# GRU graph layers on one core: preparation of tiles 4 to 7 spaced evenly and split, the last tiles' results written as x + m z h - m (z - 1) n, the last chain in halves

## The chip, the core and the metric

The kernel runs on 1 core of one Trainium2 chip. The metric is the device time of one execution in microseconds. Engines are named as in the profile: PE (TensorE), DVE (VectorE), ACT (ScalarE), POOL (GpSimd), SP (SyncE, which here only issues DMAs).

## What is computed

64 graphs of 128 nodes with 128 channels. The state starts as relu of a layer norm, five layers of a gated graph network follow, and the result is added to the input:

```python
h = jnp.maximum(_layernorm(x), 0.0)
A = (adj != 0)
for l in range(5):
    m = jnp.einsum('bnd,de->bne', h, weight[l])
    agg = jnp.einsum('bij,bid->bjd', A, m)
    gi = agg @ w_ih.T + b_ih;  gh = h @ w_hh.T + b_hh      # each split into r, z, n
    r = sigmoid(i_r + h_r);  z = sigmoid(i_z + h_z)
    n = tanh(i_n + r * h_n)
    h = (1.0 - z) * n + z * h
out = x + h * mask
```

## The kernel before

**Tiles and units.** A tile is 4 graphs side by side: 128 partitions (channels, or nodes) by 512 columns; there are 16. One tile through one layer is a unit; there are 80, in the order of the list `units`: groups of 4 tiles, and within a group layer by layer, so the same tile comes again 4 units later. `K` is a unit's number (0 to 79), `l` its layer, `t` its tile, `LAST` the last layer (4). Units 16 to 19, 36 to 39, 56 to 59 and 76 to 79 are last layers.

**What a unit does.** PE: three products of the state with the hidden weights (`ps_r`, `ps_z`, `ps_hn`), three of the aggregated state `s` with the folded input weights (`ps_r`, `ps_z`, `ps_in`), each as three fp16 matmuls of high and low parts, and 8 small matmuls for the next unit's aggregation (`ps_s`). ACT: `r` (L478), `z` (L484), `s_hi` of the next unit (L472), the high part of the last unit's state (L494), `n` by tanh (L488). DVE: `rhn` (L624), the sum in `ps_in` (L630), `s_lo` of the next unit (L618), then the new state in two operations (L636, L641). POOL: `zh`, the product z h (L816), and `state_low`, the low part of the last unit's state (L821). SP: a transpose of the new state's two halves, `nat<-hp` (L242), which the aggregation of the same tile's next layer reads. Each engine runs its own list in order; semaphores tie them together.

**Preparation.** Tiles 4 to 15 are prepared while others are computed. Tile `t` begins at unit `prep[t]`, and stage `s` of it runs in unit `prep[t] + s`, behind that unit's own work on each engine: 0 moments (DVE) and loads, 1 `aggregate` (DVE) and statistics `inverse_std` (POOL, four small operations), 3 and 4 `layernorm` in two pieces (ACT), 5 `natural_high` (ACT) and `natural_low` (POOL), 6 `split` (ACT, the copy to `halves`), the compare of a tile 4 to 7 (POOL) and two transposes (SP), 7 the compare of the others (DVE, `adjacency`), 8 and 9 `join` in two pieces (DVE). Two neighbours stand `gap` units apart. `prep` is 4, 7, 10, 13 for tiles 4 to 7 and 18, 23, ... 53 for 8 to 15. `v_high` and `v_low` of layers 3 and 4 (ACT, DVE) fall into units 6 and 10, and PE folds layer 4's weights behind unit 10.

**Ends.** Finished tiles are masked and added to x on POOL (`masked_result`, `final`) and stored by SP. For the last group DVE does the mask product (`masked_state`, L648) for units 76 to 78. The very last unit takes its products in the order z, r, hn, in, and computes x + m z h on POOL (`masked_last_h`, `kept_result`), and DVE subtracts m (z - 1) n (`masked_open`, `last_result`); ACT copies the mask to PSUM (`move_mask`) and issues the last store.

Of the kernel before, what the change touches and what calls it, by code (L numbers as in the profile page):

```python
# [5 lines left out]
ALU = mybir.AluOpType  # L6
# [21 lines left out]
FINISH = 3  # L28
STAGES = 10
# [7 lines left out]
def gnn_kernel(nc, x, xT, adj, mask_row, fold_lhs, w_ihT, w_hhT, bias_ih, bias_hh, ident, out):  # L37
# [10 lines left out]
    END = at[starts[-1], LAST]  # L48
# [25 lines left out]
    storing = {adds[t] + 1: t for t in ends}  # L74
    fetching = {ends[t] - FETCH: [t] for t in ends}
    fetching.setdefault(N - FINISH - FETCH, []).append(TILES - 1)

# [4 lines left out]
    with ExitStack() as ctx:  # L82
# [66 lines left out]
        ps_s, ps_t, ps_f = bank("ps_s"), bank("ps_t"), bank("ps_f")  # L149

# [64 lines left out]
        def _(sp):  # L215
# [16 lines left out]
            def transpose_halves(t):  # L232
                sp.wait_ge(split_done, t - FIRST + 1)
# [39 lines left out]
            for K in range(1, N + 2):  # L273
# [6 lines left out]
                if K in tile_at_stage[6]:  # L280
                    transpose_first(tile_at_stage[6][K])
                    transpose_halves(tile_at_stage[6][K])
                if K in storing:
                    store(storing[K])
                for t in fetching.get(K, ()):
                    load_ends(t)
            for f in range(FRING):
                sp.wait_ge(stored[f], 16 * len(range(f, TILES, FRING)))

        @block.tensor  # L290
        def _(pe):
# [24 lines left out]
            def h_products(K):  # L316
# [29 lines left out]
            def last_products(K):  # L346
                pe.wait_ge(s_lo_done, K + 1)
                s_product(K, 1, ps_z).then_inc(z_mm, 1)
                s_product(K, 0, ps_r).then_inc(r_mm, 1)
# [85 lines left out]
        def _(act):  # L435
# [26 lines left out]
            def split(t):  # L462

                act.wait_ge(h0_done, 2 * t + 2)
                if t - FIRST >= 2:
                    act.wait_ge(halves_loaded[t % 2], 16 * ((t - FIRST) // 2))
                nc.scalar.copy(halves[:, t % 2], h0[:, t % LN].bitcast(U16).rearrange("p (c b) -> p b c", b=2)).then_inc(
                    split_done, 1)
# [16 lines left out]

            def gate_n(K):
# [13 lines left out]
            def move_mask():  # L500

                f = (TILES - 1) % FRING
                act.wait_ge(ends_loaded[f], 32 * ((TILES - 1) // FRING + 1))
                act.wait_ge(s_lo_done, N)
                nc.scalar.copy(ps_s[:], mask_in[:, f]).then_inc(mask_moved, 1)
# [35 lines left out]
            for K in range(N):  # L541
# [8 lines left out]
                else:  # L550
                    gate_z(K)
                    gate_r(K)
                    move_mask()
# [368 lines left out]
```

## Time and profile before

| | |
|---|---|
| median of 3 runs | 371.98 us (371.85 to 372.28) |
| the profiled execution, its own time | 371.11 us |
| its span, first to last instruction | 369.2 us |
| busy: PE, DVE, ACT, POOL | 98%, 87%, 81%, 71% of the span |
| mean granted TensorE clock | 0.997 |
| HBM read, written | 17.57 MB, 4.19 MB |

The span is what the rows below lie in; the execution's own time is 1.9 us longer. A matmul's row shows 0.38 us for 512 columns, longer than the distance to the next, because matmuls are pipelined. In the rows, a bracket at the end gives the engine's idle time ahead of the instruction and what ended it.

### The profile page before, as it was taken

The page shows a single profiled execution, that of the slowest core. Times are in us where ns is not written, and L with a number is a line of the kernel's source. Part 1 is how long each engine was busy: PE and PEld are TensorE (multiplying, and loading weights), DVE is VectorE, ACT ScalarE, POOL GpSimd, SP SyncE. Part 2 cuts the span into 40 slices and gives each one's busy share as a digit, 9 for nine tenths or more (in the row PEclk, how much of TensorE's full clock was granted, in tenths as well). Part 3 has the DMA queues.
Part 4 walks back from the last instruction along what each step waited for, and adds up shares of the span by engine and source line. Part 5 has one row for each costly group of instructions (what it writes and reads, how often), then busy time and mean ns, then how long its engine had stood idle before and what let it go on. Part 6 is the DMA issues. An engine that isn't in the chain of part 4 may idle for free.

```text
span 369.2 us, 6528 instructions
## 1 busy us (share of the span) xinstructions
PE 360.0 (98%) x2125; PEld 181.1 (49%) x2125; DVE 322.8 (87%) x588; ACT 299.8 (81%) x495; POOL 263.6 (71%) x261
## 2 busy tenths in 40 slices
PE   7999999999999999999999999999999999999992
PEld 3455555544454555555545455555545555555541
DVE  4977898899889999999999999999998988787886
ACT  5997788998879988888877889899877767777753
POOL 3765758889578878787656878888756777755574
PEclk9999999999999999999999999999999999999998
DMA  8634443857662693939624384756834543349522
GB/s 245 211 59 86 115 97 76 170 126 151 152 115 45 147 180 78 228 68 200 169 42 105 64 197 85 164 123 158 151 94 112 130 99 59 89 100 231 124 57 85
DMA packets 108512, 46.03 MB, mean 125 GB/s; under 512 B 97728, under 2 KB 98112, under 8 KB 108480
## 3 DMA queue, kind: packets, MB, share of 16 engines
q1 hardware_dynamic: 108336, 45.37, 55.3%
q8 instruction: 17, 0.28, 0.3%
q10 hardware_dynamic: 144, 0.26, 0.2%
q14 instruction: 15, 0.12, 0.1%
HBM read 17.57 MB, written 4.19 MB: 59 GB/s over the span
## 4 chain that ended last, share of the span: by engine, by line
PE 90%; DVE 4%; DMA 2%; POOL 2%; issue 1%; ACT 1%; DVEq 0%; POOLq 0%
PE ps_r L293 9%; PE ps_z L294 9%; PE ps_z L293 9%; PE ps_r L294 9%; PE ps_z L295 9%; PE ps_r L295 9%; PE ps_s L366 5%; PE ps_s L367 5%; PE ps_in L295 4%; PE ps_hn L294 4%; PE ps_in L293 4%; PE ps_in L294 4%; PE ps_hn L295 4%; PE ps_hn L293 4%; DMA hp<-nat 1%
## 5 line engine op out<-in xcount | busy, mean ns | idle before, releaser
L816 POOL TENSOR_TENSOR zh<-z,h 128x512 f32<-128x512 f32 x80 | 101.9, 1273 | 81.4 <-ACT z L484 81.3
L478 ACT ACTIVATE r<-ps_r,b_sum,unscale 128x512 f32<-128x512 f32 x80 | 62.2, 778 | 37.9 <-PE ps_r L295 37.5
L488 ACT ACTIVATE ps_in<-ps_in,b_ih,unscale 128x512 f32<-128x512 f32 x80 | 60.1, 751 | 22.3 <-DVE ps_in L630 21.3
L821 POOL TENSOR_TENSOR hp<-h,hp 128x512 f16<-128x512 f32 x64 | 74.1, 1157 | 0.0
L624 DVE SCALAR_TENSOR_TENSOR rhn<-ps_hn,b_hn,r 128x512 f32<-128x512 f32 x80 | 59.8, 748 | 10.3 <-ACT r L478 9.8
L630 DVE TENSOR_TENSOR ps_in<-ps_in,rhn 128x512 f32<-128x512 f32 x80 | 56.0, 700 | 11.5 <-PE ps_in L295 6.7
L484 ACT ACTIVATE z<-ps_z,b_sum,unscale 128x512 f32<-128x512 f32 x80 | 61.6, 770 | 0.7 <-PE ps_z L295 0.7
L641 DVE TENSOR_TENSOR h<-zh,ps_in 128x512 f32<-128x512 f32 x76 | 52.2, 687 | 8.5 <-DVE ps_in L636 0.5
L636 DVE SCALAR_TENSOR_TENSOR ps_in<-z,ps_in 128x512 f32<-128x512 f32 x79 | 54.7, 692 | 5.6 <-ACT ps_in L488 5.6
L618 DVE TENSOR_TENSOR s_lo<-ps_s,s_hi 128x512 f16<-128x512 f32 x80 | 54.4, 680 | 0.4 <-ACT s_hi L472 0.4
L472 ACT CAST s_hi<-ps_s 128x512 f16<-128x512 f32 x80 | 46.6, 583 | 0.0
L366 PE MATMUL ps_s<-a,nat 128*128 128x128 f16 x320 | 44.3, 219 | 0.0
L367 PE MATMUL ps_s<-a,nat 128*128 128x128 f16 x320 | 44.3, 219 | 0.0
L494 ACT CAST hp<-h 128x512 f16<-128x512 f32 x64 | 40.7, 635 | 0.1
L366 PEld LDWEIGHTS ps_s<-a,nat 128*128 128x128 f16 x320 | 31.3, 98 | 9.4 <-POOL nat L804 0.4
L367 PEld LDWEIGHTS ps_s<-a,nat 128*128 128x128 f16 x320 | 31.3, 98 | 9.0
L293 PE MATMUL ps_z<-s_hi,v_hi 128*128 128x512 f16 x80 | 30.3, 379 | 0.5 <-DVE s_lo L618 0.5
L293 PE MATMUL ps_r<-s_hi,v_hi 128*128 128x512 f16 x80 | 30.4, 380 | 0.2 <-DVE s_lo L618 0.2
L293 PE MATMUL ps_r<-hp,u_hi 128*128 128x512 f16 x79 | 30.0, 379 | 0.5 <-DMA hp<-nat 0.2
L294 PE MATMUL ps_r<-s_lo,v_hi 128*128 128x512 f16 x80 | 30.3, 379 | 0.0
L295 PE MATMUL ps_r<-s_hi,v_lo 128*128 128x512 f16 x80 | 30.3, 379 | 0.0
L294 PE MATMUL ps_z<-s_lo,v_hi 128*128 128x512 f16 x80 | 30.3, 379 | 0.0
(115 smaller groups left out, 745.0 us busy)
## 6 DMA issues: line engine op xcount, KB each, us to landing
x_in<-in_x SPq DMA_DIRECT2D x16, 256.0 KB, 3.8
adj_in<-in_adj SPq DMA_DIRECT2D x16, 256.0 KB, 3.4
x_out<-in_xT SPq DMA_DIRECT2D x16, 256.0 KB, 3.1
mask_in<-in_mask_row SPq DMA_DIRECT2D x16, 256.0 KB, 3.8
out<-x_out SPq DMA_DIRECT2D x15, 256.0 KB, 2.7
nat<-hp SPq DMA_TRANSPOSE x64, 3.1
fold_in<-in_fold_lhs SPq DMA_DIRECT2D x1, 320.0 KB, 3.9
out<-x_out ACTq DMA_DIRECT2D x1, 256.0 KB, 2.1
```

Source lines behind the costliest of these rows:

```text
L293: nc.tensor.matmul(ps[:], w_hi, m_hi, start=start, stop=False)
L294: nc.tensor.matmul(ps[:], w_hi, m_lo, start=False, stop=False)
L295: return nc.tensor.matmul(ps[:], w_lo, m_hi, start=False, stop=stop)
L366: nc.tensor.matmul(block_of(ps_s, q), block_of(nat_hi(t), q), a_q, start=True, stop=False)
L367: last = nc.tensor.matmul(block_of(ps_s, q), block_of(nat_lo(t), q), a_q, start=False, stop=True)
L478: nc.scalar.activation(r[:], ps_r[:], ACT.Sigmoid, bias=b_sum[:, 0:1], scale=unscale[:, 0:1]).then_inc(r_done, 1)
L484: nc.scalar.activation(z[:, K % 2], ps_z[:], ACT.Sigmoid, bias=b_sum[:, 1:2], scale=unscale[:, 0:1]).then_inc(z_done, 1)
L488: nc.scalar.activation(ps_in[K % 2][:], ps_in[K % 2][:], ACT.Tanh, bias=b_ih[:, 2:3], scale=unscale[:, 0:1]).then_inc(n_done, 1)
L624: nc.vector.scalar_tensor_tensor(out=rhn[:], in0=ps_hn[:], scalar=b_hn[:, 0:1], in1=r[:], op0=ALU.add, op1=ALU.mult).then_inc(rhn_done, 1)
L630: nc.vector.tensor_tensor(ps_in[K % 2][:], ps_in[K % 2][:], rhn[:], ALU.add).then_inc(npre_done, 1)
L816: nc.gpsimd.tensor_tensor(zh[:, K % 2], z[:, K % 2], h[:, t % RING], ALU.mult).then_inc(zh_done, 1)
L821: nc.gpsimd.tensor_tensor(h_lo(t), h[:, t % RING], h_hi(t), ALU.subtract).then_inc(h_lo_done, 1)
```

## The change

1. *Preparation.* Nine stages instead of ten, tiles 4 to 7 four units apart: `prep` is 2, 6, 10, 14 for tiles 4 to 7 and 19, 24, ... 54 for 8 to 15. For tiles 4 to 7 the moments stand two units ahead of `prep` (units 0, 4, 8, 12). `layernorm` is at stages 2 and 3, `natural_high` at 4, `split` in two pieces at 4 and 5, transposes and POOL's compare at 5, DVE's compare at 6, `join` at 7 and 8.
2. *Ends.* Units 76 and 77 are masked on POOL like other tiles. Units 78 and 79 both go by x + m z h - m (z - 1) n. In unit 79 the products come r, z, hn, in, and from the tanh on it works in two halves of 256 columns in `last_n` (`ps_f`, `ps_s`); SP stores the first half and ACT the second.
3. Fetching and storing times in `ends` move with `prep`; the inputs of tiles 14 and 15 are fetched before those of 12 and 13.

```diff
-FINISH = 3
-STAGES = 10
+FINISH = 4
+STAGES = 9
...
-    END = at[starts[-1], LAST]
+    END = N - 2
...
-        gap = 3 if t < starts[1] + GROUPS[1] else SPREAD
+        gap = 4 if t < starts[2] else SPREAD
...
+    measured = {prep[t] - (2 if t < starts[2] else 0): t for t in prep}
...
+        last_n = (ps_f, ps_s)
+        last_mask = (ps_f, ps_t)
...
+            sp.wait_ge(last_out, 1)
+            sp.dma_start(out_t[TILES - 2], x_out[:, (TILES - 2) % FRING]).then_inc(stored[(TILES - 2) % FRING], 16)
+            sp.wait_ge(last_out, 2)
+            sp.dma_start(half_of(out_t[TILES - 1], 0), half_of(x_out[:, (TILES - 1) % FRING], 0)).then_inc(
+                stored[(TILES - 1) % FRING], 16)
...
-            def split(t):
+            def split(t, half):
...
+                act.wait_ge(h0_done, 2 * t + 1 + half)
...
+            def last_gate_n(K, half):
+                act.wait_ge(npre_done, K + 1)
+                nc.scalar.activation(last_n[half][:, 0:TILE // 2], half_of(ps_in[K % 2], half), ACT.Tanh, bias=b_ih[:, 2:3],
+                                     scale=unscale[:, 0:1]).then_inc(n_done, 1)
...
+                if K in (N - 4, N - 3):
+                    move_mask(K - N + TILES + 2)
...
+            def last_open_n(K, half):
+
+                dve.wait_ge(n_done, K + 1 + half)
+                dve.wait_ge(open_done, 2)
+                n = last_n[half][:, 0:TILE // 2]
+                nc.vector.tensor_tensor(n, half_of(mask_in[:, units[K][0] % FRING], half), n, ALU.mult).then_inc(zn_done, 1)
+
+            def last_result(K, half):
+
+                dve.wait_ge(zn_done, K + 1 + half)
+                dve.wait_ge(last_kept, 2)
+                result = half_of(x_out[:, units[K][0] % FRING], half)
+                nc.vector.tensor_tensor(result, result, last_n[half][:, 0:TILE // 2], ALU.subtract).then_inc(last_out, 1)
...
-                if 0 < K < N - 1:
+                if 0 < K < END:
                     new_state(K)
+                elif K == END:
+                    masked_open(K)
+                    open_n(K)
+                    result(K)
                 elif K:
                     masked_open(K)
-                    last_result(K)
-                if END <= K < N - 1:
-                    masked_state(K)
+                    last_open_n(K, 0)
+                    last_open_n(K, 1)
+                    last_result(K, 0)
+                    last_result(K, 1)
...
+                if END > K - 1 >= at[starts[-1], LAST]:
+                    masked_result(units[K - 1][0])
                 kept(K)
-                if K == N - 1:
+                if K >= END:
                     kept_result(K)
-                    final(TILES - 2)
...
-                if K == N - FINISH:
-                    masked_last_h()
+                if K in (N - FINISH - 1, N - FINISH):
+                    masked_last_h(K - N + FINISH + TILES - 1)
```

How the lists of three engines change. First ACT, from the tanh of unit 13 on, before (`h<-x_in` is a layernorm piece, `halves<-h` is `split`):

```order
L488 ACTIVATE ps_in<-ps_in,b_ih,unscale 128x512
L442 ACTIVATE h<-x_in,shift,rstd 128x128 x2
L467 COPY halves<-h 128x1024
L478 ACTIVATE r<-ps_r,b_sum,unscale 128x512
L484 ACTIVATE z<-ps_z,b_sum,unscale 128x512
L472 CAST s_hi<-ps_s 128x512
L494 CAST hp<-h 128x512
L488 ACTIVATE ps_in<-ps_in,b_ih,unscale 128x512
L442 ACTIVATE h<-x_in,shift,rstd 128x128 x2
L478 ACTIVATE r<-ps_r,b_sum,unscale 128x512
```

and in the changed kernel, from the tanh of unit 14 on (`nat<-h` is `natural_high`):

```order
L503 ACTIVATE ps_in<-ps_in,b_ih,unscale 128x512
L459 ACTIVATE nat<-h 128x512
L476 COPY halves<-h 128x2x256
L488 ACTIVATE r<-ps_r,b_sum,unscale 128x512
L494 ACTIVATE z<-ps_z,b_sum,unscale 128x512
L482 CAST s_hi<-ps_s 128x512
L509 CAST hp<-h 128x512
L503 ACTIVATE ps_in<-ps_in,b_ih,unscale 128x512
L476 COPY halves<-h 128x2x256
L488 ACTIVATE r<-ps_r,b_sum,unscale 128x512
```

Layernorm pieces and the copy no longer meet in one unit; a half copy stands behind `natural_high`, and the other in the next unit.

Then POOL, before, from `zh` of unit 10 on (`a<-adj_in` is the compare; `var_eps`, `rstd`, `minus_mean` and `shift` are the statistics):

```order
L816 TENSOR_TENSOR zh<-z,h 128x512
L821 TENSOR_TENSOR hp<-h,hp 128x512
L800 TENSOR_SCALAR a<-adj_in 128x512
L816 TENSOR_TENSOR zh<-z,h 128x512
L821 TENSOR_TENSOR hp<-h,hp 128x512
L786 TENSOR_TENSOR var_eps<-mean_var,eps 128x4
L788 TENSOR_TENSOR rstd<-var_eps,neg_half 128x4
L790 TENSOR_TENSOR minus_mean<-mean_var,neg_one 128x4
L796 TENSOR_TENSOR shift<-minus_mean,rstd 128x4
L816 TENSOR_TENSOR zh<-z,h 128x512
```

and in the changed kernel, from `zh` of unit 7 on:

```order
L855 TENSOR_TENSOR zh<-z,h 128x512
L860 TENSOR_TENSOR hp<-h,hp 128x512
L825 TENSOR_TENSOR var_eps<-mean_var,eps 128x4
L827 TENSOR_TENSOR rstd<-var_eps,neg_half 128x4
L829 TENSOR_TENSOR minus_mean<-mean_var,neg_one 128x4
L835 TENSOR_TENSOR shift<-minus_mean,rstd 128x4
L839 TENSOR_SCALAR a<-adj_in 128x512
L855 TENSOR_TENSOR zh<-z,h 128x512
L860 TENSOR_TENSOR hp<-h,hp 128x512
L855 TENSOR_TENSOR zh<-z,h 128x512
```

Statistics of tile 5 and the compare of tile 4 now stand together between `zh` of unit 7 and `zh` of unit 8; so do those of the next tiles in units 11 and 15.

Last, the end of DVE's list before, from `rhn` of unit 78:

```order
L624 SCALAR_TENSOR_TENSOR rhn<-ps_hn,b_hn,r 128x512
L630 TENSOR_TENSOR ps_in<-ps_in,rhn 128x512
L618 TENSOR_TENSOR s_lo<-ps_s,s_hi 128x512
L636 SCALAR_TENSOR_TENSOR ps_in<-z,ps_in 128x512
L641 TENSOR_TENSOR ps_in<-zh,ps_in 128x512
L648 TENSOR_TENSOR mask_in<-mask_in,ps_in 128x512
L624 SCALAR_TENSOR_TENSOR rhn<-ps_hn,b_hn,r 128x512
L630 TENSOR_TENSOR ps_in<-ps_in,rhn 128x512
L656 SCALAR_TENSOR_TENSOR mask_in<-z,ps_s 128x512
L664 TENSOR_TENSOR ps_in<-mask_in,ps_in 128x512
L667 TENSOR_TENSOR x_out<-x_out,ps_in 128x512
```

and in the changed kernel, from `s_lo` of unit 79:

```order
L640 TENSOR_TENSOR s_lo<-ps_s,s_hi 128x512
L672 SCALAR_TENSOR_TENSOR mask_in<-z,ps_f 128x512
L679 TENSOR_TENSOR ps_in<-mask_in,ps_in 128x512
L687 TENSOR_TENSOR x_out<-x_out,ps_in 128x512
L646 SCALAR_TENSOR_TENSOR rhn<-ps_hn,b_hn,r 128x512
L652 TENSOR_TENSOR ps_in<-ps_in,rhn 128x512
L672 SCALAR_TENSOR_TENSOR mask_in<-z,ps_t 128x512
L694 TENSOR_TENSOR ps_f<-mask_in,ps_f 128x256
L694 TENSOR_TENSOR ps_s<-mask_in,ps_s 128x256
L701 TENSOR_TENSOR x_out<-x_out,ps_f 128x256
L701 TENSOR_TENSOR x_out<-x_out,ps_s 128x256
```

The mask product of L648 has gone, two operations on whole tiles have become four on halves, and unit 78 has three operations where it had three. What left DVE stands on POOL, whose list ends, changed, from `masked_last_h` of tile 15 on, with

```order
L876 TENSOR_TENSOR h<-mask_in,h 128x512
L866 TENSOR_TENSOR mask_in<-mask_in,h 128x512
L855 TENSOR_TENSOR zh<-z,h 128x512
L871 TENSOR_TENSOR x_out<-x_out,mask_in 128x512
L866 TENSOR_TENSOR mask_in<-mask_in,h 128x512
L855 TENSOR_TENSOR zh<-z,h 128x512
L882 TENSOR_TENSOR x_out<-x_out,zh 128x512
L871 TENSOR_TENSOR x_out<-x_out,mask_in 128x512
L855 TENSOR_TENSOR zh<-z,h 128x512
L882 TENSOR_TENSOR x_out<-x_out,zh 128x512
```

where `mask_in<-mask_in,h` is `masked_result` of tiles 12 and 13 and `x_out<-x_out,mask_in` is `final` of the same tiles.

## Rows read from the trace of the kernel before

**Rows 1.** Timeline, PE: last matmul into `ps_in` of units 14, 15, 18 and 76 (start us, us).

```profile
79.78 0.38 PE L295 MATMUL ps_in<-s_hi,v_lo 128*128 128x512 f16 x1
84.59 0.38 PE L295 MATMUL ps_in<-s_hi,v_lo 128*128 128x512 f16 x1
98.11 0.38 PE L295 MATMUL ps_in<-s_hi,v_lo 128*128 128x512 f16 x1
349.40 0.38 PE L295 MATMUL ps_in<-s_hi,v_lo 128*128 128x512 f16 x1
```

**Rows 2.** Timeline, units 13 to 15: ACT, PE and PE's weight loads.

```profile
77.66 0.87 ACT L442 ACTIVATE h<-x_in,shift,rstd 128x128 f32<-128x128 f32 x2
78.43 1.03 ACT L467 COPY halves<-h 128x1024 uint16<-128x1024 uint16 x1
79.37 0.78 ACT L478 ACTIVATE r<-ps_r,b_sum,unscale 128x512 f32<-128x512 f32 x1
80.29 0.38 PE L293 MATMUL ps_r<-hp,u_hi 128*128 128x512 f16 x1
82.40 0.10 PEld L293 LDWEIGHTS ps_r<-s_hi,v_hi 128*128 128x128 f16 x1 [0.51 <-DVE s_lo L618]
```

**Rows 3.** Timeline, a unit without side work: ACT, POOL, DVE and PE.

```profile
348.07 0.78 ACT L478 ACTIVATE r<-ps_r,b_sum,unscale 128x512 f32<-128x512 f32 x1 [1.10 <-PE ps_r L295]
349.60 1.27 POOL L816 TENSOR_TENSOR zh<-z,h 128x512 f32<-128x512 f32 x1 [1.95 <-ACT z L484]
350.42 0.68 DVE L618 TENSOR_TENSOR s_lo<-ps_s,s_hi 128x512 f16<-128x512 f32 x1
351.56 0.38 PE L293 MATMUL ps_r<-s_hi,v_hi 128*128 128x512 f16 x1
```

**Rows 4.** Timeline, POOL and DVE: a DVE copy beside POOL; `zh` after statistics.

```profile
72.62 1.17 POOL L821 TENSOR_TENSOR hp<-h,hp 128x512 f16<-128x512 f32 x1
72.73 1.38 DVE L676 COPY h<-halves_t 128x512 uint16<-128x512 uint16 x1
73.74 1.35 POOL L804 TENSOR_TENSOR nat<-h,nat 128x512 f16<-128x512 f32 x1
128.64 1.28 POOL L816 TENSOR_TENSOR zh<-z,h 128x512 f32<-128x512 f32 x1 [0.20 <-ACT z L484]
```

**Rows 5.** Groups by line: two operations of tile preparation (busy us, mean ns | idle before).

```profile
L450 ACT ACTIVATE nat<-h 128x512 f16<-128x512 f32 x16 | 9.9, 621 | 0.0
L800 POOL TENSOR_SCALAR a<-adj_in 128x512 f16<-128x512 f32 x4 | 7.9, 1978 | 0.0
```

**Rows 6.** The page's sixth part: DMA issues, with median us to landing.

```profile
nat<-hp SPq DMA_TRANSPOSE x64, 3.1
```

**Rows 7.** The chain that ended last, in order of time (start us, us, what).

```profile
352.13 0.71 DVE ps_in L641
352.93 0.69 DVE mask_in L648
```

**Rows 8.** Timeline, the last unit and the two last stores.

```profile
359.57 0.68 DVE L618 TENSOR_TENSOR s_lo<-ps_s,s_hi 128x512 f16<-128x512 f32 x1
360.31 0.39 PE L293 MATMUL ps_z<-s_hi,v_hi 128*128 128x512 f16 x1 [0.53 <-DVE s_lo L618]
362.02 1.28 POOL L816 TENSOR_TENSOR zh<-z,h 128x512 f32<-128x512 f32 x1 [1.26 <-ACT z L484]
362.69 0.74 DVE L624 SCALAR_TENSOR_TENSOR rhn<-ps_hn,b_hn,r 128x512 f32<-128x512 f32 x1
365.90 0.33 SPq L253 DMA_DIRECT2D out<-x_out  x1
366.50 0.37 ACTq L510 DMA_DIRECT2D out<-x_out  x1
```

**Rows 9.** Stretches of the end: busy us (x instructions) by engine, PEclk, DMA share, GB/s.

```profile
366.50:367.00 0.50, 0.00 (x0) 0.00 (x0) 0.00 (x0) 0.00 (x0) 0.00 (x0) 1.00 0.53 205
368.00:368.50 0.50, 0.00 (x0) 0.00 (x0) 0.00 (x0) 0.00 (x0) 0.00 (x0) 0.50 0.25 90
```

More of the change, by code:

```diff
@@ L73, in gnn_kernel @@
     adding = {adds[t]: t for t in ends if t < TILES - 2}
-    storing = {adds[t] + 1: t for t in ends}
-    fetching = {ends[t] - FETCH: [t] for t in ends}
-    fetching.setdefault(N - FINISH - FETCH, []).append(TILES - 1)
+    storing = {adds[t] + 1: t for t in ends if t < TILES - 2}
+    fetching = {ends[t] - FETCH: [t] for t in ends if t < TILES - 2}
+    for K, t in enumerate((TILES - 2, TILES - 1), N - FINISH - 1):
+        fetching.setdefault(K - FETCH, []).append(t)
     xT_t = xT.rearrange("d (t c) -> t d c", c=TILE)
@@ L183, in block_of, with half_of @@
             return tile_ap[:, q * P:(q + 1) * P]
+        def half_of(tile_ap, half):
+            return tile_ap[:, half * TILE // 2:(half + 1) * TILE // 2]
         def h_hi(t):
@@ L347, in last_products @@
                 pe.wait_ge(s_lo_done, K + 1)
+                s_product(K, 0, ps_r).then_inc(r_mm, 1)
                 s_product(K, 1, ps_z).then_inc(z_mm, 1)
-                s_product(K, 0, ps_r).then_inc(r_mm, 1)
                 pe.wait_ge(rhn_done, K)
@@ L498, in v_high, with move_mask @@
                 nc.scalar.activation(v_hi[:, l], folded(l)[:, 0:CG], ACT.Copy, scale=scale[:, 0:1]).then_inc(v_hi_done, 1)
[L500 to L505, printed above, removed]
+            def move_mask(t):
+                f = t % FRING
+                act.wait_ge(ends_loaded[f], 32 * (t // FRING + 1))
+                act.wait_ge(v_lo_done, L)
+                nc.scalar.copy(last_mask[t % 2][:], mask_in[:, f]).then_inc(mask_moved, 1)
             def store_last():
                 t = TILES - 1
-                act.wait_ge(last_out, 1)
-                act.dma_start(out_t[t], x_out[:, t % FRING]).then_inc(stored[t % FRING], 16)
+                act.wait_ge(last_out, 3)
+                act.dma_start(half_of(out_t[t], 1), half_of(x_out[:, t % FRING], 1)).then_inc(stored[t % FRING], 16)
             def squares(weights, begin, sums):
@@ L550, in _ @@
                 else:
+                    gate_r(K)
                     gate_z(K)
[L552 to L553 removed]
                 if K == 1:
@@ L641, in new_state, with open_n, result @@
                 nc.vector.tensor_tensor(out_ap, zh[:, K % 2], ps_in[K % 2][:], ALU.subtract).then_inc(h_done, 1)
[L643 to L648 removed]
             def masked_open(K):
[L652 removed]
+                t = units[K][0]
+                f = t % FRING
                 dve.wait_ge(z_done, K + 1)
[L654 to L656 removed]
+                dve.wait_ge(last_h_masked, K - END + 1)
+                dve.wait_ge(mask_moved, K - END + 1)
+                nc.vector.scalar_tensor_tensor(out=mask_in[:, f], in0=z[:, K % 2], scalar=1.0, in1=last_mask[t % 2][:],
                                                op0=ALU.subtract, op1=ALU.mult).then_inc(open_done, 1)
[L659 to L661 removed]
+            def open_n(K):
                 dve.wait_ge(n_done, K + 1)
                 dve.wait_ge(open_done, 1)
[L664 removed]
+                nc.vector.tensor_tensor(ps_in[K % 2][:], mask_in[:, units[K][0] % FRING], ps_in[K % 2][:],
+                                        ALU.mult).then_inc(zn_done, 1)
+            def result(K):
+                f = units[K][0] % FRING
                 dve.wait_ge(zn_done, K + 1)
@@ L755, in _ @@
                     adjacency(3)
-                if K in tile_at_stage[0]:
-                    moments(tile_at_stage[0][K])
+                if K in measured:
+                    moments(measured[K])
                 if K in tile_at_stage[1]:
                     aggregate(tile_at_stage[1][K])
-                if K in tile_at_stage[7] and not pool_compares(tile_at_stage[7][K]):
-                    adjacency(tile_at_stage[7][K])
+                if K in tile_at_stage[6] and not pool_compares(tile_at_stage[6][K]):
+                    adjacency(tile_at_stage[6][K])
                 for half in range(2):
-                    if K in tile_at_stage[8 + half]:
-                        join(tile_at_stage[8 + half][K], half)
+                    if K in tile_at_stage[7 + half]:
+                        join(tile_at_stage[7 + half][K], half)
                 if K == 0:
```

79 lines of the change are left out of this document (32 added, 47 removed).

## Prediction

> **What bounds the kernel now.** I read the timeline of PE first, taking one fixed event of every unit: the start of the last matmul into `ps_in`, which I call the unit's mark. From unit 18 to unit 76 the marks lie 251.29 us apart over 58 units, 4.333 us each [rows 1]. A unit is 18 matmuls of 512 columns and 8 of 128 columns, so 20 pitches of 0.217 us: PE runs back to back there and nothing on another engine matters as long as it keeps up. So a gain can come only from where marks lie further apart, and from what follows the last matmul.
>
> There are two such places behind the start. Unit 15's mark comes 4.81 us after unit 14's, and unit 18's comes 13.52 us after unit 15's where three units take 13.00 [rows 1]: 0.48 + 0.52 = 1.00 us lost. Then the tail: the last unit's products start at 360.31 after an idle wait for `s_lo`, and 6.2 us pass from there to the last issue of a store, at 366.50 [rows 8].
>
> Why unit 15 is late stands in the timeline. In unit 13 ACT does two layernorm pieces and the copy to `halves`, from 77.66 to 79.46, 1.80 us [rows 2], where a unit without side work leaves ACT 1.10 us before `r` [rows 3]. On pace, `r` starts 1.33 us ahead of its unit's mark (348.07 against 349.40 [rows 1, 3]), thus at 78.45; it started at 79.37, 0.92 late. It ended at 80.15, and PE's next product into `ps_r`, due 0.22 after the mark at 80.00, started at 80.29 [rows 2]. So `r` may be 0.92 - 0.29 = 0.63 us late for nothing. The other 0.19 is DVE's: the weight load of the s-products at 82.40 waited for `s_lo` [rows 2]; DVE had moments and a `join` in unit 14's neighbourhood. The slack of `s_lo` on pace is 0.46: it ends at 351.10 and is used at 351.56 [rows 3]. Unit 18 is the same picture one tile later.
>
> **Preparation of tiles 4 to 7.** Nothing is removed; work of 4 tiles moves to units with room. ACT: layernorm halves (0.87 a pair) now stand alone in a unit. The copy of 1.03 becomes two; each costs between 0.52 (half) and 1.03 (no gain from halving). I take 0.6, near the 0.62 of a 128x512 copy [rows 5]. The first stands behind `natural_high`, 0.62: 1.2 in a unit against 1.10. Units 6 and 10 also hold a `v_hi` copy, at most 0.62 more, so 1.8 less overlap: `r` of unit 7 is about 0.5 late, inside 0.63; unit 11 has a fold matmul's delay as further room. At 1.03 a half, `r` would be 0.9 late in unit 7 and cost 0.3.
>
> DVE: the moments (four pieces) move two units ahead and no longer meet a `join`. In unit 0 they stand ahead of `v_low(1)`, which waits for ACT anyway. The price of a `join` isn't its own length: in the timeline one began at 72.73, 0.11 after POOL's `state_low`, and ended at 74.11, 0.32 behind POOL's end at 73.79, while POOL's next instruction ran 0.18 longer than the one before it [rows 4]. So a `join` costs until POOL's current instruction ends, and one `join` a unit leaves `s_lo` inside its 0.46, since later tiles do exactly that between marks 18 and 76 at full pace. For the same reason `aggregate` ahead of `adjacency` in one unit (tiles 8 to 14) is free: it fills time in which the compare would wait for POOL.
>
> POOL is where something is given back. A unit leaves it 1.95 us idle ahead of `zh` [rows 3]; statistics leave 0.20 of that [rows 4], so cost 1.75; a compare costs 1.98 [rows 5]. Both now stand in units 7, 11 and 15, where before they stood apart. So `zh` of units 8, 12, 16 is 1.75 + 1.98 - 1.95 = 1.8 late. It ends 0.20 + 1.27 + 1.8 = 3.3 behind the mark; its user, the new state, is due 2.73 behind it (352.13 less 349.40 [rows 1, 7]), 3.2 when moments stand ahead. That is 0.1 and DVE has room. Queued behind `zh` is `state_low`, and on it hangs the transpose to `nat` on SP. On pace it ends 0.20 + 1.27 + 1.17 = 2.6 behind the mark and the transpose lands 3.1 later [rows 3, 4, 6], 5.7. PE needs it for the aggregation three units on, that is 2 x 4.33 - 0.87 = 7.8 behind that mark. Slack 2.1, less 1.8, is 0.3; in unit 8, where z is another 0.4 late from unit 6's ACT work, it is 0. Queued on SP ahead of it are the two transposes of tile 4, issued 3 us earlier, which may lengthen the landing. I charge 0.2 in all, between 0 and 0.9 (0.3 a time). Early part: 1.00 - 0.2 = 0.8 us won, 0.1 to 1.0.
>
> **Tiles 8 to 15** start one unit later and end at the same one; the marks are on pace there before, so at best nothing is won. I take 0.05 lost, for `join`s beside a mask product, between 0 and 0.4.
>
> **The tail.** Before, `mask_in` on DVE (0.69 [rows 7]) stands behind the new state of units 76, 77 and 78, and DVE falls behind PE. After, for 76 and 77 POOL has it, in its 1.95 of idle time, and DVE stays on pace: `s_lo` of the last unit at 350.42 + 2 x 4.33 = 359.08 instead of 359.57 [rows 3, 8]. The s-products start at 360.31 - 0.49 = 359.82. The `hn` product is the ninth matmul: eight pitches of 0.217 and one matmul's own 0.38 [rows 1] later it is out, 361.94. `r`, now first, is ready before that (359.82 + 2 x 0.217 + 0.38 + 0.78 = 361.4), and DVE is through with unit 78's result, three operations of 0.7 behind `s_lo`, at 361.9. So `rhn` of unit 79 starts at 361.96 (0.02 for the semaphore) instead of 362.69 [rows 8]: 0.73 won. The mask copies on ACT (two of 0.6) delay only the tanh of unit 76, by 0.4, and DVE has 0.4 idle.
>
> From `rhn` on, the chain was 366.50 - 362.69 = 3.81 long. The halves cut the tanh by some 0.2, but DVE's mask product, then four half operations of 0.35 to 0.69, stand where two whole ones did: between +1.3 and -0.2. I take 0, because POOL holds the same moment: its `zh` of unit 79 comes behind a mask product, `zh` 78, `kept_result`, and `final` of tile 13, in a row from the new state of unit 77 at 357.2: 4 x 1.27 gives 362.3 against 362.02 before [rows 8], and 2 x 1.27 more is 364.9, when the first half wants it. The second half is out at 365.8.
>
> Then the stores. Two of 256 KB were issued at 365.90 and 366.50 [rows 8]; their data ran from about 366.7 to about 368.1 [rows 9]; the span ended at 369.20, 2.7 behind the last issue. After, tile 14's has gone 4 us earlier, tile 15's first half 0.35 earlier, and one of 128 KB stands at the end. At no less than the 205 GB/s of the half-busy stretch [rows 9] it moves in 0.4 to 0.6 us, where the two together took 1.4: issue to end between 1.7 and 2.7, I take 2.2, 0.5 won. Tail: 0.73 + 0.5 = 1.2 us, 0.6 to 1.8.
>
> **Sum.** 0.8 - 0.05 + 1.2 = 1.95. Span 369.20 to 367.25, profiled execution 371.11 to 369.15; the median shown, 371.98, lies 0.87 above that execution, so 370.0.
>
> **Rivals.** (a) *Only the tail wins*: POOL's statistics and compare make a transpose late in units 7, 11, 15, and half copies cost their whole length: 0.9 + 0.3 against the 1.0 won. 371.98 - 1.2 + 0.2 = 371.0. For it: the slack of 0.3. Against: landings of 3.1 with a free queue. 18%. (b) *The tail's gain is eaten by POOL*: six POOL operations follow the new state of 77; 0.2 more each is 1.2 later, and 371.98 - 0.8 = 371.2. For it: one ran 1.35 instead of 1.17 beside a `join` [rows 4]; against: none is near the end. 7%. (c) *The early change only shifts the stalls*, say to units 6 to 11, and the tail wins only its store: 371.98 - 0.5 = 371.5, no change by the bound. 5%. (d) *Slower, by one mechanism*: DVE's compare doesn't slip in between POOL's instructions. For tiles 8 to 14, `aggregate` frees POOL's statistics just as the compare queues. If the compare waited for that whole group, 1.75, less the slack of 0.46, seven times, 9 us would be lost and the end would be near 379; it decides from a wait of about 0.75 on. Against it stands the row of 74.11, where the copy ended 0.32 behind one POOL instruction though the next was queued [rows 4]. 4%.
>
> The Trainium skill (SBUF — State Buffer, Who interferes with whom) says that such a copy and a POOL instruction exclude one another for a whole instruction and that issue order decides. By that rule the trace agrees, 0.32 behind POOL's end, and the sum above stays as it is. It says nothing on who wins among queued ones, so (d) keeps its small chance.
>
> **Chances.** Forecast 66%, (a) 18, (b) 7, (c) 5, (d) 4. The measurement tells from no change what exceeds about 0.2%, 0.74 us. Faster (below 371.2): 66 + 18 + half of (b) and a little, 0.89; same 0.07; slower 0.04. The forecast's own bounds are 369.2 (early 1.0, tail 1.8) and 370.7; with (a) and most of (b) 369.2 to 371.1 holds eight in ten.
>
> **What would show it.** Marks of units 14 to 18 at 4.33 apart; `join`s not beside moments; no matmul of `ps_s` that waits for `nat` at units 10, 14 and 18 (rival a); `s_lo` of the last unit 1.02 behind the mark of unit 78, its products about 0.5 earlier against that mark; `rhn` to the last issue about 3.8; last issue to end about 2.2. Wrong I am if a new stall shows at units 6 to 11, if marks between 19 and 60 spread, or if the last `x_out` operation waits for POOL.

## The result, and the profile after

The changed kernel takes 374.17 us (median; 373.08 to 374.79) against 372.13 us before, measured beside it. The ratio is 1.0054, 95% interval 1.0035 to 1.0072: slower by half a per cent, where 370.0 and faster was predicted. The profiled execution took 373.08 us, its span is 371.1.

The marks say at once where. This is the timeline of PE in the changed kernel, last matmul into `ps_in` of units 17, 18 and 19, of 26 and 27, and of 78 and 79:

```profile
93.16 0.38 PE L308 MATMUL ps_in<-s_hi,v_lo 128*128 128x512 f16 x1
97.49 0.38 PE L308 MATMUL ps_in<-s_hi,v_lo 128*128 128x512 f16 x1
101.85 0.38 PE L308 MATMUL ps_in<-s_hi,v_lo 128*128 128x512 f16 x1
...
132.17 0.38 PE L308 MATMUL ps_in<-s_hi,v_lo 128*128 128x512 f16 x1
137.53 0.38 PE L308 MATMUL ps_in<-s_hi,v_lo 128*128 128x512 f16 x1
...
360.95 0.38 PE L308 MATMUL ps_in<-s_hi,v_lo 128*128 128x512 f16 x1
365.10 0.38 PE L308 MATMUL ps_in<-s_hi,v_lo 128*128 128x512 f16 x1
```

Units 15 to 18 now stand 4.33 apart: the 1.00 us of [rows 1] has been won. But unit 27 comes 5.36 behind unit 26, and so come 32 (4.57), 37 (4.77) and 57 (6.18): 1.03 + 0.24 + 0.44 + 1.85 = 3.56 us lost, at places that were on pace before. In what follows a *stall* at a unit is this: what its distance from the unit before exceeds 4.33 by.

The page's fifth part has PE's groups by line (busy us, mean ns, then idle us before them and its releaser). The group of the aggregation's first products has idle time of its own, and the timeline puts it at three places, in units 27, 37 and 57 (in unit 32 only the weight load ahead of the product waited, 0.55):

```profile
L375 PE MATMUL ps_s<-a,nat 128*128 128x128 f16 x320 | 44.4, 219 | 2.8 <-DMA nat<-hp 2.8
```

```profile
136.64 0.23 PE L375 MATMUL ps_s<-a,nat 128*128 128x128 f16 x1 [0.85 <-DMA nat<-hp]
180.62 0.23 PE L375 MATMUL ps_s<-a,nat 128*128 128x128 f16 x1 [0.27 <-DMA nat<-hp]
269.10 0.23 PE L375 MATMUL ps_s<-a,nat 128*128 128x128 f16 x1 [1.67 <-DMA nat<-hp]
```

PE waits for the transposed state, `nat`. What made it late is in the chain that ended last, in order of time (start us, us, what), from 128 us on:

```profile
128.04 0.59 SPq L232
...
128.67 0.43 SPq L227
...
129.15 1.24 SPq L238
...
130.49 1.28 SPq L244
...
131.83 0.86 SPq L261
...
132.73 3.86 DMA nat<-hp
136.59 0.05 issue
136.64 0.23 PE ps_s L375
```

The chain runs for 4.7 us through nothing but SP issuing: load of `adj` (L232), load of `x` (L227), `transpose_first` (L238), `transpose_halves` (L244), a store (L261), and only then the state's transpose, at 132.73. What that one waits for, POOL's `state_low`, had long ended:

```profile
129.27 1.16 POOL L860 TENSOR_TENSOR hp<-h,hp 128x512 f16<-128x512 f32 x1
```

It ended at 130.43, so the transpose was issued 2.3 us late, and landed 3.86 later where the median is 3.1. Before the change the loads (stage 0) and the transposes (stage 6) of tiles 8 to 15 stood in different units. With the transposes at stage 5 and tiles 5 units apart, stage 0 of one tile and stage 5 of the tile before fall on one unit; the store came onto it too, because the ends are put in phase with `prep`, which moved by one.

The tail: first the mark of unit 78 in the kernel before, then the changed kernel from `s_lo` of the last unit on:

```profile
358.06 0.38 PE L295 MATMUL ps_in<-s_hi,v_lo 128*128 128x512 f16 x1
...
361.98 0.68 DVE L640 TENSOR_TENSOR s_lo<-ps_s,s_hi 128x512 f16<-128x512 f32 x1
362.71 0.39 PE L306 MATMUL ps_r<-s_hi,v_hi 128*128 128x512 f16 x1
364.94 0.75 DVE L646 SCALAR_TENSOR_TENSOR rhn<-ps_hn,b_hn,r 128x512 f32<-128x512 f32 x1
366.53 0.54 ACT L498 ACTIVATE ps_f<-ps_in,b_ih,unscale 128x256 f32<-128x256 f32 x1 [1.51 <-DVE ps_in L652]
366.58 1.26 POOL L882 TENSOR_TENSOR x_out<-x_out,zh 128x512 f32<-128x512 f32 x1
367.94 0.42 DVE L701 TENSOR_TENSOR x_out<-x_out,ps_f 128x256 f32<-128x256 f32 x1
368.39 0.33 SPq L298 DMA_DIRECT2D out<-x_out  x1
368.73 0.37 ACTq L526 DMA_DIRECT2D out<-x_out  x1
```

`rhn` of unit 79 starts 3.99 behind unit 78's mark (before 4.63, [rows 8] and the mark at 358.06), the last issue is 3.79 behind `rhn` (3.81), the span ends 2.37 behind the last issue (2.70). In all the end is 10.15 behind unit 78's mark, and was 11.14: 0.99 us won.

I add the stretches up for all kernels of this study from their marks (us; "to 0" is the mark of unit 0, which varies between profiled executions by over a us, among kernels with the same code up to there as well, so spans alone mislead):

| kernel | span | to 0 | 0 to 11 | 11 to 19 | 19 to 78 | 78 to end | stalls behind unit 11 (unit: us over 4.33) |
|---|---|---|---|---|---|---|---|
| before | 369.2 | 16.47 | 50.30 | 35.68 | 255.61 | 11.14 | 15: .48, 17: .09, 18: .44 |
| changed | 371.1 | 16.86 | 50.31 | 34.68 | 259.10 | 10.15 | 27: 1.03, 32: .24, 37: .44, 57: 1.85 |
| e1_loads | 369.4 | 16.86 | 50.28 | 34.72 | 257.44 | 10.10 | 14: .06, 57: 1.85 |
| e2_phase | 368.7 | 16.57 | 50.30 | 35.32 | 256.39 | 10.12 | 18: .66, 27: .78 |
| e3_both | 367.6 | 16.86 | 50.30 | 34.65 | 255.62 | 10.17 | none over .03 |
| e4_before_collide | 375.9 | 16.81 | 50.30 | 35.65 | 262.04 | 11.10 | 15, 17, 18 as before; 27: 1.55, 32: .60, 37: .50, 57: 2.14, 58: 1.69 |
| e5_tail | 369.6 | 16.53 | 50.53 | 36.77 | 255.62 | 10.15 | 15: .49, 16: .51, 17: .67, 18: .45 |
| e6_swap | 366.9 | 16.10 | 50.29 | 34.67 | 255.71 | 10.13 | 58: .11 |
| e7_thin | 371.2 | 17.27 | 50.28 | 34.90 | 258.57 | 10.18 | 14: .22, 27: .93, 37: .10, 57: 1.98 |
| e8_whole | 368.0 | 17.11 | 50.28 | 34.85 | 255.61 | 10.15 | 18: .19 |

### The profile page after: what moved, and what is told of

It reads as the page before. It is cut to its first block, busy times and chain, and to the rows that moved or that the text cites. A ratio compares the mean times of both kernels' runs of the same rounds, so it can differ in the third digit from the quotient of the medians.

```text
span 371.1 us, 6561 instructions
## 1 busy us (share of the span) xinstructions
PE 360.1 (97%) x2125; PEld 181.6 (49%) x2125; DVE 320.4 (86%) x588; ACT 301.9 (81%) x509; POOL 265.9 (72%) x264
## 4 chain that ended last, share of the span: by engine, by line
PE 74%; POOL 8%; SPq 6%; DMA 6%; issue 2%; DVE 2%; ACT 1%; DVEq 0%; POOLq 0%
PE ps_r L306 7%; PE ps_z L308 7%; PE ps_r L307 7%; PE ps_z L307 7%; PE ps_z L306 7%; PE ps_r L308 7%; DMA nat<-hp 4%; PE ps_s L375 4%; PE ps_s L376 4%; PE ps_hn L308 4%; PE ps_hn L306 4%; PE ps_hn L307 4%; PE ps_in L308 4%; PE ps_in L307 4%; PE ps_in L306 4%; POOL hp L860 2%
## 5 line engine op out<-in xcount | busy, mean ns | idle before, releaser
L663 DVE TENSOR_TENSOR h<-zh,ps_in 128x512 f32<-128x512 f32 x78 | 53.6, 688 | 9.3 <-POOL zh L855 1.1
L308 PE MATMUL ps_z<-s_hi,v_lo 128*128 128x512 f16 x80 | 30.3, 379 | 0.0
```

What stands on the lines that cost most here:

```text
L308: return nc.tensor.matmul(ps[:], w_lo, m_hi, start=False, stop=stop)
```

## The experiments

A *fetch* is the pair of loads of `x_out` and `mask_in` for a tile that ends soon; a *landing* is the time from a transfer's issue to its end. The theory, S: loads, transposes of prepared tiles, stores and fetches that meet in one unit of SP's in-order list hold back the state's transpose behind them. Rivals: P, POOL is what is late (`natural_low` and `final` now stand in one unit, and `state_low` of unit 23 ends 3.2 us behind the mark of unit 24, where 2.6 is the pace, so that SP starts that unit's list 0.65 late); C, contention: the transfers that now run together lengthen the transpose's landing (3.86 and, at unit 54, 4.40, against 3.1).

### Taking the meeting apart: e1_loads, e2_phase, e3_both

In the changed kernel, e1 moves the loads two units on:

```
-                if K in tile_at_stage[0]:
-                    load_adj(tile_at_stage[0][K])
+                if K in tile_at_stage[2]:
+                    load_adj(tile_at_stage[2][K])
...
```

> The changed kernel, with the loads of adjacency and x two units later (prep + 2), so that they no longer stand on SP in the unit in which a tile's two extra transposes and a store are issued. Theory S (SP's list: loads 1.1 us, two transposes 2.6 us and a store 0.6 to 0.9 us are issued ahead of the transpose of unit 24's new state and of its like every five units, which goes out 2.3 us after it could): the transpose goes out 1.1 us earlier, the stall of 1.03 at unit 27 goes and that of 1.85 at unit 57 falls below 0.8; 374.2 falls to 370.5 to 372.5. Theory P (POOL has natural_low and final in one unit, and state_low is late): no change, 374.2. Theory C (the transpose lands late because of the bytes of the stores and loads around it, whatever the order of issue): the time from issue to landing falls from 3.9 and 4.4 to about 3.1, and the time with it.

e2 moves the ends (and with them `final`, stores and fetches) by one unit in their period of five:

```
-            ends[t] += (prep[TILES - 1] + 3 - ends[t]) % SPREAD
+            ends[t] += (prep[TILES - 1] + 2 - ends[t]) % SPREAD
```

> The changed kernel with one number changed: the ends of finished tiles (mask product, addition, store, fetching) one unit earlier, so that final stands a unit ahead of natural_low on POOL and the store a unit ahead of the two transposes on SP, as in the kernel before. The loads still stand with the transposes. Theory S: the transpose goes out 0.6 to 0.9 us earlier, stalls fall to half or less, 371 to 372.5. Theory P: state_low is on time and all stalls go, 370.0. Theory C: less traffic beside the transpose, 371 to 372.5.

e3 does both.

> Both edits at once: neither loads nor stores with the transposes. Theory S: the transpose goes out when the two other transposes are issued, 0.7 us late at most, no stall behind unit 18, 370.0 (369.5 to 370.6), which is what the blind sum gave. Theories P and C: the same time, reached by e2 alone (P).

Measured against a kernel before of 371.91 us: e1 371.33, ratio 0.998 (0.9964 to 0.9995); e2 370.21, 0.9951 (0.9932 to 0.997); e3 369.54, 0.9945 (0.9926 to 0.9963). In e1 POOL's list is that of the changed kernel, and `state_low` of unit 23 is as late as there (3.23 behind the mark in both), yet the stalls at 27, 32 and 37 are gone. P alone is refuted. But the state's transpose of unit 24 also landed sooner, in 3.1 us instead of 3.86, which is what theory C had expected.

What is left is unit 57. SP's issues in e1 and the last piece of the chain there:

```profile
258.08 1.27 SPq L238 DMA_TRANSPOSE hp<-nat  x1
259.45 1.28 SPq L244 DMA_TRANSPOSE halves_t<-halves  x1
260.78 0.57 SPq L261 DMA_DIRECT2D out<-x_out  x1
261.40 0.43 SPq L256 DMA_DIRECT2D x_out<-in_xT  x1
261.88 0.45 SPq L257 DMA_DIRECT2D mask_in<-in_mask_row  x1
...
262.37 5.02 DMA nat<-hp
```

A store and a fetch meet the transposes there, once, without a load. The expectation that this stall would fall below 0.8 failed: it stayed at 1.85. The transpose did go out earlier (1.97 us behind the end of its `state_low` instead of 2.58), but it landed in 5.02 us instead of 4.40, and the one made up for the other.

In e2, with loads but no store in the unit, 0.78 at unit 27 and 0.66 at unit 18 are left. At 370.21 us e2 is nearer to what theory P expected (370.0, all stalls gone) than to the 371 to 372.5 of S and C; the stall at unit 27, with POOL less late, speaks against P alone. The chain of e2 shows the three pieces that matter:

```profile
92.94 3.97 DMA nat<-hp
...
130.35 2.17 SPq L244
...
132.57 4.12 DMA nat<-hp
```

At unit 24 the store was gone, but the issue of `transpose_halves` took 2.17 where it took 1.28 in the changed kernel, so that SP's list was as long as with the store (4.67 against 4.69): its start, 0.5 us less late behind POOL, is all that e2 won there. From unit 29 on the transposes went out 0.8 us earlier and more. The stall at unit 18 is no meeting on SP: its transpose was issued 0.03 behind POOL's `state_low` of unit 15, which was late (4.39 behind the mark), and landed in 3.97. That is the mechanism of the prediction's rival (a).

With both moved, no stall is left between units 12 and 78. e3 is faster than both kernels, and so are e2 and, below, e6 and e8; their intervals do not tell them apart (0.9944 to 0.9951).

### The same meeting in the kernel before: e4_before_collide

In before's code the loads of tiles 8 on stand one unit later, the ends one unit later in their period; everything else is before's, the tail too.

```
+    tile_at_stage_m = {prep[t] + (1 if t >= 8 else 0): t for t in prep}
...
-                if K in tile_at_stage[0]:
-                    load_adj(tile_at_stage[0][K])
+                if K in tile_at_stage_m:
+                    load_adj(tile_at_stage_m[K])
...
-            ends[t] += (prep[TILES - 1] + 3 - ends[t]) % SPREAD
+            ends[t] += (prep[TILES - 1] + 4 - ends[t]) % SPREAD
```

> The kernel before, with loads one unit later and the ends one unit later for tiles 8 on, so that SP's list has the order of the changed kernel there (loads, two transposes, store, then the state's transpose) and POOL has natural_low with final. Everything else, the copy to halves in one piece and the tail among it, is before's. Theory S (and P): stalls on PE at units near 27, 32, 37 and 57 as in the changed kernel, 372.1 rises by 2 to 4.5 to 374 to 376.5. If the stalls came from split copies, aggregate with adjacency in one unit, or the nine stages themselves: 372.1, unchanged.

Measured: 375.61 us, ratio 1.0103 (1.0072 to 1.0134), as theories S and P expected. Stalls appear at 27, 32, 37, 57 and, new, 58: 6.4 us between marks 19 and 78 in the profiled execution, which was the slowest of six (377.87 us). Those of before at 15, 17 and 18 stay. So the meeting makes the loss without the split copy, the shorter preparation or the new tail. It is a meeting on two engines, though: `final` stands with `natural_low` on POOL too, and `state_low` of unit 24 ended 3.14 behind its mark where it is 2.59 in the changed kernel. Nearly all of the difference at unit 27, a stall of 1.55 against 1.03, comes from that 0.55.

The 1.69 at unit 58 is of another kind. No transfer was late there; PE had just stood idle for 1.96 us, at unit 57, and from about 272.1 to 275.5 it ran at the lower of its two clocks (1.2 instead of 2.4 GHz). The stretch's row gives busy us of PE, PEld, DVE, ACT and POOL, then the granted clock:

```profile
271.26 0.23 PE L367 MATMUL ps_s<-a,nat 128*128 128x128 f16 x1 [1.96 <-DMA nat<-hp]
272.20:275.50 3.30, 3.30 (x9) 1.16 (x8) 2.57 (x5) 1.84 (x4) 0.49 (x1) 0.50 0.35 105
```

So this stall cost almost as much again behind it. In the changed kernel the wait of 1.67 at unit 57 left the clock at 1.00.

### Issue order or transfers: e6_swap and e7_thin

Both start from the changed kernel. e6 lets SP issue a unit's loads, store and fetches behind the next state's transpose instead of ahead of it:

```
-                if K in tile_at_stage[0]:
+                if K in tile_at_stage[1]:
...
-                if K in storing:
-                    store(storing[K])
-                for t in fetching.get(K, ()):
+                if K - 1 in storing:
+                    store(storing[K - 1])
+                for t in fetching.get(K - 1, ()):
```

> The changed kernel with a swap in SP's list alone: in each unit the loads, the store and the fetches stand behind the next state's transpose instead of ahead of it; each transfer moves by less than a unit, bytes and the other engines' lists are the same. Theory S (issue order on SP delays the state's transpose): what stands ahead of it shrinks from 4.8 to 2.5 us in units 23, 28 and so on, its issue is 2.3 us earlier, the stalls at units 27, 32, 37 and 57 go, 370.0 or ratio 0.995. Theory C (contention: the loads' and the store's data lengthen the transpose's landing): they now move at the very time that the transpose does, its landing stays at 3.9 or more, and the stalls stay or grow, 373.5 to 375, ratio 1.004 or above. Theory P (POOL's state_low is 0.65 late in units with natural_low and final, and that decides): no change in the stalls, ratio 1.005.

e7 keeps every instruction of SP at its place and leaves out 15/16 of the loads' bytes, of `adj` from tile 8 on and of `x` from tile 12 on in the same way, so that the results of these tiles are not the right ones:

```
+                part = slice(0, TILE if t < 8 else TILE // 16)
-                sp.dma_start(adj_in[:, t % ADJ], adj[t])...
+                sp.dma_start(adj_in[:, t % ADJ, part], adj[t][:, part])...
```

> The changed kernel with 1/16 of the columns in the loads of adj for tiles 8 on and of x for tiles 12 on; the rest of these buffers keeps older tiles' data, so the later tiles' results are other ones. Same instructions on SP, same order, hardly any bytes from the loads. Theory S: the stalls at 27, 32, 37 and 57 stay within 0.3 us of 3.56 in all, ratio 1.005. Theory C: they go, ratio 0.995 to 0.997. In between (issue order makes 2.3 of delay, contention the 0.8 by which the landing is longer than 3.1): the stalls shrink by 0.8 each, leaving some 0.2 at 27 and 1.0 at 57, ratio 0.998.

Measured, against 372.06 us: e6 369.62, ratio 0.9944 (0.9924 to 0.9964); e7 373.00, ratio 1.0035 (1.002 to 1.005). In e6 SP's issues stand so:

```profile
125.98 1.23 SPq L250 DMA_TRANSPOSE nat<-hp  x1
127.25 1.33 SPq L238 DMA_TRANSPOSE hp<-nat  x1
128.69 1.28 SPq L244 DMA_TRANSPOSE halves_t<-halves  x1
130.01 1.34 SPq L250 DMA_TRANSPOSE nat<-hp  x1
131.41 0.57 SPq L232 DMA_DIRECT2D adj_in<-in_adj  x1
132.02 0.44 SPq L227 DMA_DIRECT2D x_in<-in_x  x1
132.51 0.43 SPq L261 DMA_DIRECT2D out<-x_out  x1
```

The state's transpose goes out at 130.01, 0.4 behind the end of `state_low` (128.48 + 1.15 = 129.63), and the loads and the store run right beside it; the stalls at 27, 32, 37 and 57 are gone. One of 0.11 is left, at unit 58. In e7 hardly any bytes are loaded, and the stalls are there, 3.01 us at units 27, 37 and 57 where there were 3.56; within 0.3 of 3.56 had been expected, so the bytes may account for a small part. At unit 24 the store behind the loads was issued in 0.57 us instead of 0.86, for one. The chain of e7 shows the landings:

```profile
133.05 4.05 DMA nat<-hp
264.55 4.57 DMA nat<-hp
```

They are not shorter than with the loads' bytes (3.86 and 4.40). This decides against C as far as the loads' bytes go.

**What a stall is made of.** Three times add up, from the mark of one unit to the landing of the state's transpose: until POOL's `state_low` ends, from there to the issue on SP, and the landing. PE feels it only when the sum is over 7.73 us: sum less 7.73 gives every stall of this table to 0.02 (sums are of unrounded times).

| kernel, unit of the stall | `state_low` behind the mark | to the issue | landing | sum | stall |
|---|---|---|---|---|---|
| changed, 27 | 2.59 | 2.31 | 3.86 | 8.75 | 1.03 |
| changed, 32 | 2.59 | 2.18 | 3.20 | 7.96 | 0.24 |
| changed, 37 | 2.59 | 1.88 | 3.70 | 8.17 | 0.44 |
| changed, 47 | 2.58 | 1.61 | 3.27 | 7.46 | 0 |
| changed, 57 | 2.59 | 2.58 | 4.40 | 9.57 | 1.85 |
| e1, 57 | 2.58 | 1.97 | 5.02 | 9.57 | 1.85 |
| e2, 18 | 4.39 | 0.03 | 3.97 | 8.39 | 0.66 |
| e2, 27 | 2.58 | 1.81 | 4.12 | 8.51 | 0.78 |
| e4, 27 | 3.14 | 2.18 | 3.96 | 9.28 | 1.55 |
| e6, 27 | 2.58 | 0.38 | 3.36 | 6.32 | 0 |
| e6, 58 | 2.59 | 0.03 | 5.22 | 7.83 | 0.11 |
| e7, 27 | 2.58 | 2.03 | 4.05 | 8.66 | 0.93 |
| e7, 57 | 2.58 | 2.55 | 4.57 | 9.70 | 1.98 |
| e8, 18 | 4.23 | 0.03 | 3.66 | 7.92 | 0.19 |

So the late issue is needed for the loss of the changed kernel: with 0.03 in the second column its longest sum would be 7.02. But it is not the whole of it: with the median landing of 3.1 its four stalls would be 0.27, 0.14, 0 and 0.54, about 1 us of 3.56. The rest hangs on landings that were longer than the median where SP's list was crowded, and e6, which cures the issue, has short ones at these places too (3.36 and 3.33 for units 24 and 54). What lengthens a landing stays open. It is not the loads' bytes (e7), and two transposes ahead are not enough (3.1 in e1 at unit 24). Of the landings in these crowded units, the four directly behind a fetch (all of unit 54) are the longest: 4.40, 4.57 (e7), 4.63 (e4) and 5.02 (e1). In e1 one directly behind the loads of `adj` and `x`, with no other transpose within 2 us, took 5.1 (issue at 60.44); unit 11, which needs it, was no later than in the other profiles.

### What the tail is worth alone: e5_tail

The changed kernel with before's `STAGES`, gap, stages and whole copy to `halves`:

```
-STAGES = 9
+STAGES = 10
...
-        gap = 4 if t < starts[2] else SPREAD
+        gap = 3 if t < starts[1] + GROUPS[1] else SPREAD
...
```

> Before's order of preparation and of stores in all units, with the tail of the changed kernel (result of unit 78 open, halves in unit 79, r ahead of z, two masked results on POOL). If tail and preparation are independent: the stalls of before at units 15 to 18 stay (4.81 and 13.52 for three), none at 27, 32, 37, 57; mark of unit 79 about 4.15 behind that of 78; mark 78 to the end of the span 10.15 as in the changed kernel against 11.14; 1.0 us faster than before, ratio 0.9973. Rival: the tail's gain needs the later slots of fetches and masks of the changed schedule, then rhn of unit 79 stays 4.6 behind mark 78 and only 0.3 is won, ratio 0.9992.

Measured: 371.29, ratio 0.9982 (0.9967 to 0.9996), 0.1 to 1.2 us by the interval's ends. From unit 78's mark to the end it takes 10.15, the very time of the changed kernel, so the tail's 0.99 does not depend on the rest. But between units 11 and 19 it lost 1.1 us more than before's profiled execution, with a wait that was not there:

```profile
88.84 0.23 PE L375 MATMUL ps_s<-a,nat 128*128 128x128 f16 x1 [0.34 <-DMA nat<-hp]
```

SP's list is that of before there: load, load, two transposes, 79.61 to 83.74, then the state's. That one was issued about as soon as in before's profile (0.24 behind its `state_low`, before 0.16), but it landed in 5.0 us instead of 3.7:

```profile
nat<-hp SPq DMA_TRANSPOSE x1, 5.0
```

So before's own order had such a meeting (loads of tile 7 with the transposes of tile 5, both in unit 13), and with the same list the landing alone can decide whether PE waits. There is one profile of each; how often it happens is not known.

### Is the split of the copy needed: e8_whole

e3 with the copy to `halves` in one piece (1.03 instead of two of 0.61), in the second piece's unit:

```
-                if K in tile_at_stage[4]:
-                    split(tile_at_stage[4][K], 0)
                 if K in tile_at_stage[5]:
-                    split(tile_at_stage[5][K], 1)
+                    split(tile_at_stage[5][K])
```

> The version with loads and ends moved, and the copy to halves in one piece again (1.03 in place of two of 0.61), in the unit of the second piece. If the split matters by ACT's room: r is held back less than 0.63 there since the copy stands alone in its unit, nothing lost, 369.5, ratio 0.9945. If the later end of the copy (0.4) delays the halves' transpose on SP and with it the next state's transpose: stalls of 0.1 to 0.5 in units 27, 32, and so on, 370 to 372, ratio 0.996 to 1.000.

Measured: 369.97, ratio 0.9951 (0.9932 to 0.9969), beside e3's 0.9945 in another comparison: no difference that these intervals show. The early part is won as well with the copy in one piece: the wider spacing, by which the copy no longer shares its unit with two layernorm pieces, is enough for it, and the two pieces themselves are not shown to be worth anything. The stalls at units 27 and 32 that the second expectation names did not come. The one stall, 0.19 at unit 18, with a weight load of `ps_s` that waited 0.51 for `nat`, is not the copy's: SP issued that transpose 0.03 behind a late `state_low` of unit 15, as in e2.

## Why the prediction was wrong

**The step that failed** is "*Tiles 8 to 15* start one unit later and end at the same one; the marks are on pace there before, so at best nothing is won. I take 0.05 lost, for `join`s beside a mask product, between 0 and 0.4." It asked only what DVE does there. It measured 3.56 us, and the prediction's own sign, that the marks between 19 and 60 spread, is the one that came. The stage number of the transposes had changed while that of the loads had not, and the period is five: five units of distance became none. On SP, five issues of 0.59 + 0.43 + 1.24 + 1.28 + 0.86 = 4.4 us, 4.7 with what lies between, then stood ahead of the state's transpose. SP's queue was weighed in the prediction only for units 7, 11 and 15, and only for the two transposes of tile preparation. e6 shows that without this order the loss is gone, with POOL's list unchanged; e4 shows that the meeting, on SP and POOL together, brings such a loss to the kernel before.

The slack was in the text, too: for units 7 to 15 the prediction has 2.1 us between the landing on pace and PE's need (by the table above 7.73 less 2.59 and 3.1, 2.04). A list that holds the transpose back by 2.3 us, with a landing 0.8 longer, exceeds 2.1 by 1.0: unit 27's 1.03. At unit 54 the `x` load is gone (tiles 12 on need none) and a fetch is added (0.43 + 0.45): the transpose is issued 0.84 behind the mark of the unit before the stall where it was 0.56 at unit 27, and lands 0.54 later after its issue, 4.40. 1.03 + 0.28 + 0.54 = 1.85, as measured. The units from 39 to 49 have neither `x` load nor fetch there and lost nothing (sums of 7.46 and 7.57 for units 44 and 49; units 36 to 39 are last layers, whose state is not transposed). The issue lengths and the slack were at hand from before; the order of SP's list was not walked through unit by unit. The longer landings were less plain: before's transposes of the state land in 3.1 at the median and 4.5 at most, and with 3.1 the sum would have found about 1 us of the 3.56.

**Early part, right in kind.** The 1.00 us at units 15 to 18 went, as forecast, and in the changed kernel's profile nothing was given back: rival (a)'s late transpose in units 7, 11 and 15 came, without a stall. POOL's `state_low` of unit 11 shows it:

```profile
74.58 1.16 POOL L860 TENSOR_TENSOR hp<-h,hp 128x512 f16<-128x512 f32 x1
```

It ends at 75.74, 4.24 behind unit 12's mark at 71.50 where 2.6 is the pace, 1.6 late where 1.8 was computed, and the slack of 2.1 held it. That was partly luck. The other profiles with this part of the changed schedule lost 0.06 (e1, unit 14), 0.66 (e2, unit 18), 0 (e3), 0 (e6), 0.22 (e7, unit 14) and 0.19 (e8, unit 18) in the same way, when the landing was 3.5 to 4.0 instead of 3.1: 0.16 on average over the seven, so the 0.2 charged for it was about right. By e3 against e5, which lost 1.1 us more than before's profile in that stretch, the early part is worth 0.37% of 372, 1.4 us, with an uncertainty of about 0.9 from the two intervals; forecast 0.8. The half copy took 0.61, as taken.

**Tail, right.** 0.99 against 1.2: `rhn` 0.64 earlier against unit 78's mark (forecast 0.73), 3.79 from there to the last issue (3.8), 2.37 behind the last issue (2.2; this and `rhn` are the terms that were off, by 0.17 and 0.09). Rival (b) didn't decide: POOL's last operation ends at 367.84, and DVE's, which needs it, starts at 367.94 behind its own chain. There was nothing to spare.

**Rivals.** (a)'s mechanism is real but costs less than its 1.2 (0 to 0.66, as above). (c) and (d) did not happen; (d)'s side, slower, came by another mechanism than any that was named. With loads and ends moved, e3 has 369.54 us: the prediction's 370.0 is about the time of the change without its meeting on SP.

The Trainium skill (DMA: Bandwidth & Descriptors, Issuing engines are not separate DMA queues) says that the sequencer's time to start a DMA is usually small against the DMA itself. Here the measurement differs: an SP transpose holds its queue for 1.24 us of the 3.1 that it needs to land. Such times, added up, delayed the state's transpose by 1.6 to 2.6 us behind its input.

## What to carry to other kernels

When a stage of a periodic schedule moves, write the stages of all tiles modulo the period for every queue, SP's too: two entries whose distance becomes a multiple of the period now meet in every period, and the diff doesn't show it. In an in-order DMA list count each issue's own length as work, take the landing from crowded places and not from the median, and put the transfer on which the next compute hangs ahead of loads, stores and fetches that have units of time. A sentence that "nothing can be lost there" because that stretch is on pace needs the slack of the latest transfer, not only that of the compute engines.

## What the runs showed of the hardware that was not expected

- An issue on SP took 0.43 to 0.59 us for most loads and stores of 256 KB and 1.23 to 1.34 for most transposes; in crowded units of the changed kernel up to 1.06 for a store and 2.12 for a transpose. 1/16 of the bytes made the loads' issues no shorter: 0.59 and 0.43 at unit 24 in e7 as in the changed kernel.
- The state's transpose landed in 3.1 us at the median. Behind two others and a store it took from 3.1 (e1, unit 24) to 5.02 us (e1, unit 54, where a fetch stood between as well), with the loads' bytes or without; behind two plain loads up to 5.2 (e3, issue at 60.46).
- PE idle for 1.96 us in e4 was followed by a granted clock of 0.50 and a stall of 1.69; idle for 1.67 in the changed kernel was not.
- Unit 0's mark lay between 16.10 and 17.27 us in ten profiled executions, among the seven with the changed kernel's first units from 16.10 to 17.27: more than either part that the change won (1.00 and 0.99).
- The tanh of half a tile took 0.54 us (0.75 whole), a DVE operation on a half 0.42 (0.69 whole): a half costs 0.6 to 0.7 of a whole.
